# Cross-attention with a feed-forward block: k and the values projected in three f32r products, and the steps of a feed-forward row in another order

## The chip, the cores and the metric

The kernel runs on one core of a Trainium2 chip. The metric is the device time of one execution in microseconds (us), read as the median of several runs of the same program; lower is better.

## The reference

Eight sequences (b) of 512 rows of x and 512 rows of ctx, 256 features each. First a cross-attention with 16 heads of 16 features, then a feed-forward whose inputs and weights are rounded to a blockwise 4-bit grid:

```python
q = (layernorm(x) @ w_q.T + b_q)            # 8 x 512 x 256
k = ctx @ w_k.T + b_k
v = ctx @ w_v.T + b_v
scores = einsum('bthd,bshd->bhts', q * 0.25, k) + attn_bias   # 8 x 16 x 512 x 512
attn = softmax(where(mask, -big, scores))
x = x + (einsum('bhts,bshd->bthd', attn, v) @ w_out.T + b_out)
y = layernorm(x)
h = silu(fp4(y) @ fp4(w_gate).T) * (fp4(y) @ fp4(w_up).T)      # 704 wide
x = x + fp4(h) @ fp4(w_down).T
```

`fp4` divides every block of 16 values by its largest magnitude over 6, rounds to the grid 0, 0.5, 1, 1.5, 2, 3, 4, 6 and multiplies back. All inputs and outputs are float32.

## The kernel before, in words

Every engine has its instruction stream written out by hand; semaphores tie them together, and no scheduler reorders anything. The program has two stages.

**Attention.** An outer walk over the 8 batches, each in 32 steps `S_` (0 to 31; two halves of 16 steps, one for each group of 8 heads). In a step, TensorE makes two tiles of scores (`scores`, L1289: one f32r product of 128x512), transposes the two tiles that are four steps older (`transpose_tile`, through `transposes`, L1198: four 128x128 blocks each), and in every fourth step multiplies four older groups of probabilities by the values (`values`, L1335). Between these stand the small products of the batch. `heavy` (called after each pair of a score tile and a transposed tile) places one piece of a projection in most steps: the values in steps 0 to 7 (`make_v`, L1230), q of the next batch in steps 8 to 11 and 24 to 27 and k in steps 14, 15 and 28 to 31 (`make_qk`, L1220), the output projection of the batch before in steps 16 to 23 (L1253). A piece is one float32 product of 128x256, which the trace shows as two matmul records. `light`, at the end of a step, places the transposes of 4 blocks: of normalised x (`make_tx`), of ctx (`make_tc`, steps 9 and 13), of the attention output (`make_ot`, `make_oT`). They use PSUM banks M0 and M1 in turn, and each waits until the bank's last reader has it out.

VectorE takes the scores out of PSUM with the bias, mask and row maximum (L1060), ScalarE takes the transposed tiles out with the exponential (`exp_tile`, L767) and does a part of the subtractions (`less_max`, L774), GpSimd does the rest (L611). ScalarE also empties PSUM after the small products: `take_tc` (L713), `take_tx` (L708), `take_q` (L718), `take_k` (L723). In `step(b, S_)` these stand between the two exponentials of the step. A score tile waits until VectorE has taken the tile three before it; a transposed tile waits for the exponential of the tile two before it. `prob` is a ring of 14 tiles between L1060 and the transposes.

**Before the first score** k and q of the first heads are made in this order: transposes of ctx, weights and x on TensorE, copies out of them on ScalarE and VectorE (L780, L1043), projections, `high_k`/`high_q` on VectorE, the low parts on GpSimd, and then 24 small DMAs (`first_rows`, L393) from the queues of SyncE and ScalarE. ScalarE's copy of the value weights (L793) stands behind its 8 DMAs. VectorE then clears two slots of `stack` (L1046).

**Feed-forward.** 32 rows of 128 tokens, in `ffn_step(n)` on TensorE and ScalarE and `step(n)` on VectorE and GpSimd, as a pipeline over rows. TensorE in step n: transposes of the rounded h of row n-3 (L1198), gate and up of row n as 18 f32r products (L1529 to L1531: 12 of 128x512, 6 of 128x384), transposes of the rounded x of row n+1 (L1540), half of the down products of row n-3 (L1546, 6 records), one f32r product that makes the low part of x of row n+1 (L1556), the other half (6 records). ScalarE in step n: normalise row n+2 (`x_norm`, L862 and L866), copy of the transposed h (L890), `x_abs` of row n+2 (L882), silu of row n (L897), `x_parts` of row n+1 (L872 the high part, which L1556 waits for, and L875 the low part, which waits for L1556), absolute values of h of row n-1 (L904). VectorE's fourteen instructions of a step are L1128 to L1180, GpSimd has one (L692).

The middle rows run in a hardware loop of six steps a turn, four turns (`row_tiles`); the rest is written out.

## Time and profile before

| | before |
|---|---|
| median of 3 runs | 956.67 us (955.68 to 958.33) |
| profiled execution: its time / span from first to last instruction | 957.63 us / 955.8 us |
| mean granted TensorE clock | 0.991 |
| TensorE matmul busy | 900.2 us, 94% |
| TensorE weight loads busy | 707.5 us, 74% |
| VectorE busy | 715.0 us, 75% |
| ScalarE busy | 612.0 us, 64% |
| GpSimd busy | 534.8 us, 56% |

The times of all terms below are compared with the profiled execution: 957.63 us lie 0.96 us above the median. A matmul's busy time in the trace includes its way through the array, so that two neighbours overlap; how long TensorE is taken by an instruction is read from the distance of starts, not from its duration. Scores run from 25.9 us to about 661 us, the feed-forward rows from about 678 us to the end.

### The profile page before, as it was taken

To read this page: it belongs to the slowest core of one execution; us is meant where nothing else is said; L and a number is where in the kernel's file an instruction comes from. 1 tells how busy PE (TensorE), PEld (TensorE's weight loads), DVE (VectorE), ACT (ScalarE), POOL (GpSimd) and SP (SyncE) were. 2 spreads that over 40 slices of the span, in tenths; PEclk is the share of its full clock that TensorE was granted. 3 is DMA by queue.
4 is the path that set the end of the run, shared out by engine and by line. 5 is a ranking of instruction groups with operands and counts; after the bars stand their busy time and mean duration, and the time that the engine had idled before them with its cause. 6 is when DMAs were issued, how large, how long until landed. Compare 5 with 4: busy or idle time off the path is not lost.

```text
span 955.8 us, 20207 instructions
## 1 busy us (share of the span) xinstructions
PE 900.2 (94%) x6740; PEld 707.5 (74%) x6740; DVE 715.0 (75%) x1848; ACT 612.0 (64%) x1116; POOL 534.8 (56%) x500
## 2 busy tenths in 40 slices
PE   5799999999999999999999999898889999999997
PEld 4667778777777777777777777676667777777786
DVE  5867667677676766676766698996578888888884
ACT  3477767777777677776777778878445544444442
POOL 6777867867776686686777558854022222222222
PEclk9899999999999999999999999999989999999999
DMA  6586434334342443433435244300000000000000
GB/s 197 167 237 166 122 88 105 109 71 122 100 115 68 110 123 78 115 98 83 117 95 124 67 109 141 87 2 1 2 0 17 17 17 16 16 16 16 16 16 28
DMA packets 50792, 76.45 MB, mean 80 GB/s; under 512 B 5264, under 2 KB 22032, under 8 KB 50704
## 3 DMA queue, kind: packets, MB, share of 16 engines
q1 hardware_dynamic: 50448, 75.06, 29.5%
q8 instruction: 50, 0.82, 0.4%
q10 hardware_dynamic: 256, 0.26, 0.1%
q14 instruction: 38, 0.31, 0.1%
HBM read 45.16 MB, written 29.36 MB: 78 GB/s over the span
## 4 chain that ended last, share of the span: by engine, by line
PE 62%; issue 15%; ACT 10%; DVE 8%; POOL 1%; SPq 1%; DMA 1%; DVEq 0%; ACTq 0%; POOLq 0%
PE psum L1198 25%; PE psum L1335 12%; PE psum L1289 12%; PE psum L1220 5%; PE psum L1253 3%; PE psum L1230 2%; DVE att L1167 2%; ACT att L897 2%; ACT att L767 2%; ACT att L866 1%; ACT att L862 1%; DVE att L1138 1%; ACT att L774 1%; DVE att L1151 1%; PE psum L1556 1%
## 5 line engine op out<-in xcount | busy, mean ns | idle before, releaser
L1060 DVE CUSTOM_DVE_ANT_0 att<-psum,att 128x512 f32<-128x512 f32 x512 | 343.7, 687 | 167.4 <-PE psum L1289 166.3
L611 POOL TENSOR_TENSOR att<-att,neg_max 128x512 f32<-128x512 f32 x308 | 323.2, 1060 | 178.8 <-DVE neg_max L1060 176.2
L1198 PE MATMUL psum<-ident,att 128*128 128x128 f32 x2576 | 380.1, 275 | 24.9 <-ACT att L767 12.2
L1198 PEld LDWEIGHTS psum<-ident,att 128*128 128x128 f32 x2576 | 308.5, 141 | 95.6 <-ACT att L767 29.8
L767 ACT ACTIVATE att<-psum 128x512 f32<-128x512 f32 x512 | 299.3, 599 | 124.6 <-PE psum L1198 120.2
L1289 PE MATMUL psum<-stack 128*128 128x512 f32 x512 | 269.7, 528 | 8.5 <-DMA stack<-q_hl 6.0
L692 POOL TENSOR_TENSOR att<-att 128x704 f32<-128x704 f32 x32 | 61.6, 1927 | 182.9 <-DVE att L1176 182.9
L774 ACT ACTIVATE att<-att,neg_max 128x512 f32<-128x512 f32 x204 | 147.0, 721 | 10.3 <-DVE neg_max L1060 10.3
L1289 PEld LDWEIGHTS psum<-stack 128*128 128x128 f32 x512 | 97.7, 191 | 43.0 <-issue 31.1
L1335 PE MATMUL psum<-att 128*32 128x256 f32 x2048 | 123.8, 382 | 0.0
L1546 PE MATMUL psum<-att 128*128 128x256 f32 x384 | 92.9, 380 | 2.7 <-ACT att L890 2.7
L1335 PEld LDWEIGHTS psum<-att 128*32 128x32 f32 x2048 | 59.9, 109 | 44.6 <-issue 9.0
L882 ACT ACTIVATE att<-att 128x256 f32<-128x256 f32 x32 | 13.3, 417 | 102.6 <-DVE att L1172 102.6
L1546 PEld LDWEIGHTS psum<-att 128*128 128x128 f32 x384 | 68.5, 190 | 10.3 <-ACT att L890 3.4
L1529 PE MATMUL psum<-stack,q_hl 128*128 128x512 f32 (+1 forms) x192 | 75.6, 394 | 0.5 <-ACT q_hl L875 0.5
L1220 PE MATMUL psum<-att 128*128 128x256 f32 x256 | 74.9, 383 | 0.5
L1531 PE MATMUL psum<-stack,q_hl 128*128 128x512 f32 (+1 forms) x192 | 72.4, 377 | 0.0
L1530 PE MATMUL psum<-w_gu_low,q_hl 128*128 128x512 f32 (+1 forms) x192 | 72.3, 376 | 0.0
L1060 DVE DVE_READ_ACCUMULATOR2_ANT neg_max<- 128x1 f32 x512 | 42.2, 82 | 0.0
L1220 PEld LDWEIGHTS psum<-att 128*128 128x128 f32 x256 | 39.7, 191 | 2.9 <-ACT att L713 2.1
L730 ACT ACTIVATE att<-psum 128x512 f32<-128x512 f32 x32 | 19.1, 598 | 34.5 <-PE psum L1335 34.5
L595 POOL TENSOR_TENSOR att<-att 128x512 f32<-128x512 f32 x32 | 41.1, 1290 | 0.0
(98 smaller groups left out, 1023.0 us busy)
## 6 DMA issues: line engine op xcount, KB each, us to landing
stack<-qk_planes SPq DMA_DIRECT2D x124, 192.0 KB, 4.0
qk_planes<-k_hl SPq DMA_DIRECT2D x48, 256.0 KB
qk_planes<-q_hl SPq DMA_DIRECT2D x48, 256.0 KB
att<-in_fside_1xSxS_dram SPq DMA_DIRECT2D x32, 256.0 KB, 2.8
att<-in_ctx_dram SPq DMA_DIRECT2D x8, 512.0 KB, 6.6
out_dram<-att SPq DMA_DIRECT2D x32, 128.0 KB, 1.7
x<-in_x_dram SPq DMA_DIRECT2D x1, 2560.0 KB, 13.1
x<-in_x_dram SPq DMA_DIRECT2D x3, 512.0 KB, 7.7
```

Of the source, the lines that this page charges most:

```text
L611: pool.tensor_tensor(prob[:, slot, :], prob[:, slot, :], neg_max[:, slot:slot + 1].to_broadcast([P, S]), ALU.subtract).then_inc(less_pool, 1)
L767: act.activation(probT[:, u % 2, 2 * kk + r, :, (tt % 2) * P:(tt % 2 + 1) * P], src.rearrange("p (c t) -> p c t", c=SC), ACT.Exp, scale=1. ...
L774: act.activation(prob[:, slot, :], prob[:, slot, :], ACT.Identity, bias=neg_max[:, slot:slot + 1], scale=-1.0).then_inc(less_act, 1)
L1060: dve.tensor_tensor_reduce(out=prob[:, slot, :], in0=ps_score[:, SCORE_BANK[2 * S_ + r], :], in1=bias_m[:, tt, :], scale=-1.0, scalar=BIG, ...
L1198: return pe.transpose(out_, in_, ident[:, :])
L1220: last = pe.matmul(bank[:, cols], w_inT[:, c, which * E + o * P:which * E + (o + 1) * P], src[:, c, cols], start=c == 0, stop=c == EC - 1)
L1289: pe.matmul(ps_score[:, SCORE_BANK[j], :], stack[:, quad % SLOTS, kk, r, tt * P:(tt + 1) * P], stack[:, quad % SLOTS, kk, 2, :], start=Tru ...
L1335: last = pe.matmul(ps_O[32 * j:32 * j + 32, half * 2 * P:(half + 1) * 2 * P], vv[:, o, c, col:col + 2 * D], probT[:, u % 2, j, c, :], star ...
L1529: pe.matmul(ps_gu[:, c0:c1], f_xqT_high[:, par, c, :], w_gu_high[:, c, c0:c1], start=c == 0, stop=False)
L1530: pe.matmul(ps_gu[:, c0:c1], f_xqT_high[:, par, c, :], w_gu_low[:, c, c0:c1], start=False, stop=False)
L1531: last = pe.matmul(ps_gu[:, c0:c1], f_xqT_low[:, par, c, :], w_gu_high[:, c, c0:c1], start=False, stop=c == EC - 1)
L1546: last = pe.matmul(ps_y[:, 1 - par, :], f_hqT[:, 1 - par, c, :], w_dnT[:, c, :], start=c == 0, stop=c == IC - 1)
```

## The change

1. **k and the values.** ctx transposed and the weights of k and v are kept as a high part (rounded to f32r by ScalarE's copy) and a low part (what VectorE subtracts, `low_tc` and three subtractions at the start). A product of them is made as high x high + low x high + high x low, each an f32r product. k takes 6 products of 128x512 in the places of 4 float32 products of 128x256, a piece of `make_v` takes 3 f32r products of 128x256 in the place of one float32 product. q, the output projection and the down projection are unchanged.
2. **Places.** The second transposition of ctx moves from step 13 to step 11 and from bank M0 to M1; it waits for VectorE's low part of the first. `make_ot` moves from step 10 to step 12 and to bank M0, its `normalise` from step 11 to step 13 (in all batches but the last). `take_tc` of the second half moves from step 14 to step 12.
3. **Feed-forward.** ScalarE's step becomes: copy of the transposed h, `x_norm` of row n+3 (was n+2), silu, `x_abs` of row n+2, `x_high` of row n+1, absolute values of h, `x_low` of row n+1. VectorE's fourteen instructions stay the same and stand in another order. The loop makes three turns instead of four.
4. **Memory.** The ring of `prob` has 13 tiles instead of 14. `w_gu_low` shares the memory of the new high and low parts, `w_dnT` that of the q weights; GpSimd clears one block of it at the start.

```diff
-    RING = 14
+    RING = 13
...
-            return range(-2, 6), (6, ROWS - 2), range(ROWS - 2, ROWS + 4)
+            return range(-2, 6), (6, ROWS - 8), range(ROWS - 8, ROWS + 4)
...
             act.wait_ge(wT_ready, 2)
-            act.activation(w_inT[:, 1, 0:2 * E], psum[:, 1, :], ACT.Copy).then_inc(wT_taken, 1)
+            for c in range(EC):
+                act.activation(w_qT[:, c, :], psum[:, c, 0:E], ACT.Copy)
+                act.activation(w_kv_high[:, c, 0:E], psum[:, c, E:2 * E], ACT.Copy).then_inc(wk_high, 1)
...
-                    if S_ == 14 and not last:
-                        take_tc(b + 1, 1, M0)
+                    if S_ == 12 and not last:
+                        take_tc(b + 1, 1, M1)
...
             def ffn_step(n, par):
-                x_norm(n + 2, par)
...
-                if live(n + 2):
-                    x_abs(n + 2, par)
+                x_norm(n + 3, 1 - par)
...
+                if live(n + 2):
+                    x_abs(n + 2, par)
                 if live(n + 1):
-                    x_parts(n + 1, 1 - par)
+                    x_high(n + 1, 1 - par)
...
+                if live(n + 1):
+                    x_low(n + 1, 1 - par)
...
+            def low_tc(bp, i, bank):
+
+                dve.wait_ge(tc_taken, 2 * bp + i + 1)
+                dve.tensor_tensor(ctxT_low[:, i, :], bank, ctxT_high[:, i, :].bitcast(F32), ALU.subtract).then_inc(tc_low, 1)
...
             layernorm_stats(0, (0, 1, 2, 3))
+            for i in range(2):
+                low_tc(0, i, psum[:, 4 + i, :])
             layernorm_apply(0, (0, 1, 2, 3))
...
+            dve.wait_ge(wv_high, 1)
+            dve.tensor_tensor(w_kv_low[:, :, E:2 * E], psum[:, 1, :].rearrange("p (c e) -> p c e", c=EC), w_kv_high[:, :, E:2 * E].bitcast(F32),
+                              ALU.subtract).then_inc(wv_low, 1)
             dve.memset(stack[:, 1:SLOTS, :, :, :].bitcast(F32), 0.0).then_inc(stack_zero2, 1)
...
+                    if S_ in (10, 12) and not last:
+                        low_tc(b + 1, S_ // 12, M1)
...
+                    for j in ((0, 1), (2,), (3, 4), (5,))[piece]:
+                        c = j // 3
+                        w, y = ((w_kv_high, ctxT_high), (w_kv_high, ctxT_low), (w_kv_low, ctxT_high))[j % 3]
+                        last = pe.matmul(bank, w[:, c, o * P:(o + 1) * P], y[:, c, :], start=j == 0, stop=j == 5)
...
-                last = pe.matmul(bank[:, x * E:(x + 1) * E], ctxT[:, c, s * P:(s + 1) * P], w_inT[:, c, 2 * E:3 * E],
-                                 start=c == 0, stop=c == EC - 1)
+                for j in range(3):
+                    y, w = ((ctxT_high, w_kv_high), (ctxT_high, w_kv_low), (ctxT_low, w_kv_high))[j]
+                    last = pe.matmul(bank[:, x * E:(x + 1) * E], y[:, c, s * P:(s + 1) * P], w[:, c, E:2 * E],
+                                     start=c == 0 and j == 0, stop=c == EC - 1 and j == 2)
...
-                if S_ == 10 and not first:
+                if S_ == 11 and not last:
+                    pe.wait_ge(tc_low, 2 * b + 3)
+                    make_tc(b + 1, 1, M1)
+                if S_ == (10 if last else 12) and not first:
                     if last:
                         pe.wait_ge(v_taken, 2 * b + 2)
                     else:
-                        pe.wait_ge(tc_taken, 2 * b + 3)
-                    make_ot(4 * b - 1, M1)
-                if S_ == 13 and not last:
-                    pe.wait_ge(q_taken, 2 * b + 3)
-                    make_tc(b + 1, 1, M0)
+                        pe.wait_ge(q_taken, 2 * b + 3)
+                    make_ot(4 * b - 1, M1 if last else M0)
...
-            pe.wait_ge(wT_taken, 2)
-            pe.wait_ge(tc_taken, 2)
+
+            pe.wait_ge(wk_low, 2)
+            pe.wait_ge(tc_low, 2)
```

**VectorE, one step in the middle of the feed-forward,** before and then with the change (of 14 instructions, 12 rows with those of the registers). L1134, L1141, L1131, L1138 and L1145 of the first list are L1163, L1167, L1171, L1183 and L1190 of the second: maximum of normalised x, maximum of h, and the three roundings of x of row n+1.

```order
L1128 TENSOR_TENSOR att<-att,psum 128x704
L1131 SCALAR_TENSOR_TENSOR att<-att 128x256
L1133 REGISTER_ALU
L1134 TENSOR_REDUCE psum<-att 128x16
L1138 SCALAR_TENSOR_TENSOR att<-att 128x256
L1141 TENSOR_REDUCE psum<-att 128x44
L1145 TENSOR_TENSOR att<-att 128x256
L1151 ISA
L1151 TENSOR_TENSOR att<-psum,x 128x256
L1160 TENSOR_SCALAR att<-psum 128x60
L1161 TENSOR_SCALAR att<-psum 128x60
L1163 RECIPROCAL att<-att 128x60
```

```order
L1160 TENSOR_TENSOR att<-att,psum 128x704
L1163 TENSOR_REDUCE psum<-att 128x16
L1167 TENSOR_REDUCE psum<-att 128x44
L1171 SCALAR_TENSOR_TENSOR att<-att 128x256
L1179 TENSOR_SCALAR att<-psum 128x60
L1180 TENSOR_SCALAR att<-psum 128x60
L1183 SCALAR_TENSOR_TENSOR att<-att 128x256
L1186 RECIPROCAL att<-att 128x60
L1190 TENSOR_TENSOR att<-att 128x256
L1197 TENSOR_TENSOR att<-psum,x 128x256
L1202 SCALAR_TENSOR_TENSOR att<-att 128x704
L1207 TENSOR_TENSOR att<-att 128x256
```

The rounding of x (L1131, now L1171) moves behind both maxima, the scales and the reciprocal move ahead, and the residual sum (L1151, now L1197) moves behind the scaling of x.

**ScalarE, one step in the written-out end of the feed-forward,** before and with the change. L862/L866 (now L874/L878) are `x_norm`, L890 (L903) the copy of h, L882 (L896) `x_abs`, L897 (L909) silu, L872 (L884) and L875 (L889) the high and low part of x, L904 (L918) the absolute values of h.

```order
L866 ACTIVATE att<-att,rstd 128x256
L890 ACTIVATE att<-psum 128x768
L882 ACTIVATE att<-att 128x256
L897 ACTIVATE att<-psum 128x704
L872 ACTIVATE q_hl<-psum 128x256
L875 ACTIVATE q_hl<-psum 128x256
L904 ACTIVATE att<-att 128x704
```

```order
L903 ACTIVATE att<-psum 128x768
L874 ACTIVATE att<-x,neg_mean 128x256
L878 ACTIVATE att<-att,rstd 128x256
L909 ACTIVATE att<-psum 128x704
L896 ACTIVATE att<-att 128x256
L884 ACTIVATE q_hl<-psum 128x256
L918 ACTIVATE att<-att 128x704
L889 ACTIVATE q_hl<-psum 128x256
```

Normalising moves behind the copy of h and one row ahead, `x_abs` moves behind the silu, and the low part of x moves to the end of the step.

**ScalarE, steps 12 and 13 of a middle batch,** before and with the change. L767 (now L776) is an exponential, L774 (L783) a subtraction, L718 (L727) `take_q`, L713 (L722) `take_tc`.

```order
L718 ACTIVATE att<-psum,b_q 128x512
L774 ACTIVATE att<-att,neg_max 128x512
L767 ACTIVATE att<-psum 128x4x128 x4
L713 ACTIVATE att<-psum 128x512
L774 ACTIVATE att<-att,neg_max 128x512
```

```order
L727 ACTIVATE att<-psum,b_q 128x512
L722 ACTIVATE kv_hl<-psum 128x512
L783 ACTIVATE att<-att,neg_max 128x512
L776 ACTIVATE att<-psum 128x4x128 x4
L783 ACTIVATE att<-att,neg_max 128x512
```

The copy of ctx, which stood in step 14, now stands directly behind `take_q` and ahead of the second exponential of step 12.

## Rows read from the trace of the kernel before

**Rows 1.** Busy time by stretch: length, PE, PEld, DVE, ACT, POOL, clock, DMA.
```profile
260.00:360.00 100.00, 98.92 (x854) 76.98 (x850) 68.80 (x205) 72.18 (x130) 73.68 (x70) 1.00 0.40 104
760.00:860.00 100.00, 95.04 (x482) 77.92 (x481) 87.87 (x172) 50.88 (x102) 25.32 (x13) 1.00 0.05 16
```

**Rows 2.** Timeline (start, duration, engine), VectorE, first instruction of rows 5 and 29.
```profile
729.13 0.89 DVE L1128 TENSOR_TENSOR att<-att,psum 128x704 f32<-128x704 f32 x1
923.29 0.89 DVE L1128 TENSOR_TENSOR att<-att,psum 128x704 f32<-128x704 f32 x1
```

**Rows 3.** Timeline, one feed-forward row, all engines; in brackets idle time and releaser.
```profile
762.80 0.84 PE L1198 MATMUL psum<-ident,att 128*128 128x128 f32 x6
763.39 0.47 PE L1529 MATMUL psum<-stack,q_hl 128*128 128x512 f32 x1
763.83 0.43 DVE L1134 TENSOR_REDUCE psum<-att 128x16 f32<-128x256 f32 x1 [0.84 <-ACT att L866]
767.30 0.38 PE L1540 MATMUL psum<-ident,att 128*128 128x128 f32 x2
767.52 1.46 PE L1546 MATMUL psum<-att 128*128 128x256 f32 x6
767.97 0.42 ACT L882 ACTIVATE att<-att 128x256 f32<-128x256 f32 x1 [3.47 <-DVE att L1172]
768.29 0.74 ACT L897 ACTIVATE att<-psum 128x704 f32<-128x704 f32 x1
769.35 0.39 PE L1556 MATMUL psum<-q_hl,neg_ident 128*128 128x256 f32 x1 [0.37 <-ACT q_hl L872]
769.46 1.17 PEld L1546 LDWEIGHTS psum<-att 128*128 128x128 f32 x6
769.58 1.46 PE L1546 MATMUL psum<-att 128*128 128x256 f32 x6
770.87 0.29 PE L1198 MATMUL psum<-ident,att 128*128 128x128 f32 x1
```

**Rows 4.** Groups by line and shape: count, busy us, mean ns, idle before.
```profile
L1220 PE MATMUL psum<-att 128*128 128x256 f32 x256 | 74.9, 383 | 0.5
L1531 PEld LDWEIGHTS psum<-stack,q_hl 128*128 128x128 f32 x192 | 36.4, 190 | 5.7
```

**Rows 5.** Timeline, TensorE, first scores of batches 3 and 4.
```profile
261.44 0.50 PE L1289 MATMUL psum<-stack 128*128 128x512 f32 x1
341.54 0.50 PE L1289 MATMUL psum<-stack 128*128 128x512 f32 x1
```

**Rows 6.** Timeline, batch 3, from step 10's last transposes to step 15.
```profile
287.62 0.42 PEld L1198 LDWEIGHTS psum<-ident,att 128*128 128x128 f32 x4 [0.31 <-ACT att L713]
291.85 0.50 PE L1289 MATMUL psum<-stack 128*128 128x512 f32 x1
...
294.50 1.08 ACT L767 ACTIVATE att<-psum 128x512 f32<-128x512 f32 x2
295.15 1.09 PE L1198 MATMUL psum<-ident,att 128*128 128x128 f32 x8 [0.79 <-ACT att L767]
295.99 0.48 PE L1289 MATMUL psum<-stack 128*128 128x512 f32 x1
298.98 0.48 PE L1289 MATMUL psum<-stack 128*128 128x512 f32 x1
```

**Rows 7.** Timeline before the first scores; ACTq is ScalarE's DMA queue.
```profile
7.99 2.14 DVE L941 TENSOR_SCALAR att<-x,mean_var,rstd 128x256 f32<-128x256 f32 x4 [1.43 <-POOL rstd L566]
8.48 0.60 ACT L713 ACTIVATE att<-psum 128x512 f32<-128x512 f32 x1 [0.26 <-PE psum L1198]
17.14 5.18 DVE L1046 MEMSET stack<- 128x6144 f32 x1 [1.23 <-issue]
20.98 0.60 ACT L793 ACTIVATE att<-psum 128x512 f32<-128x512 f32 x1 [5.53 <-issue]
26.79 0.69 DVE L1060 CUSTOM_DVE_ANT_0 att<-psum,att 128x512 f32<-128x512 f32 x1 [4.47 <-PE psum L1289]
```

More of the change, by code:

```diff
@@ L1076, in body @@
                         take_v(b, S_ // 4 - 1, (M0, M1)[S_ // 4 - 1])
-                    if S_ == 11 and not first:
-                        normalise(2 * b - 1, 1, 1, M1)
+                    if S_ == (11 if last else 13) and not first:
+                        normalise(2 * b - 1, 1, 1, M1 if last else M0)
                     if S_ == 13 and not last:
@@ L1351, in heavy @@
                     if piece == 0:
[L1352 to L1357 removed]
+                        pe.wait_ge(tc_low, 2 * b + 4)
                     make_qk(1, 0, piece, M1, k_ready)
```

102 lines of the change are left out of this document (53 added, 49 removed).

## The prediction

> **What bounds the kernel now.** First the busy time by stretch [rows 1]. From 260 to 360 us TensorE is busy 98.9 of 100 us, VectorE 68.8 and ScalarE 72.2: the attention stage is TensorE's. From 760 to 860 us, in the feed-forward, TensorE shows 95.0 and VectorE 87.9: which of them bounds a row must be read from one row. So the timeline second. A row lasts 770.87 - 762.80 = 8.07 us [rows 3], and the 24 periods between the first VectorE instruction of row 5 and that of row 29 take 923.29 - 729.13 = 194.16 us, 8.09 each [rows 2]. In the same row TensorE's own work, from start to start, is 0.59 (transposes of h) + 3.91 (gate and up) + 0.22 (transposes of x) + 1.29 (six down records) + 0.23 (L1556) + 1.29 (six more) = 7.53 us. The missing 0.54 us is one wait: the first six down records start at 767.52 and are through at 768.81, and L1556 starts at 769.35, released by ScalarE's L872. VectorE's share is 87.87 / (100 / 8.07) = 7.09 us a row, with one idle piece of 0.84 us, in which it waits for ScalarE's L866. Read together these are a ring: ScalarE's L904, then `x_norm`, then VectorE from L1134 to L1172, then ScalarE's L882, which has waited 3.47 us, then silu, L872, L1556, L875 and L904 again. Neither engine is the bound there; the order is.
>
> Third, a batch of attention: 341.54 - 261.44 = 80.10 us [rows 5], the same in all middle batches. Its waits are small and local; the largest stand in steps 10 to 14 [rows 6].
>
> **Feed-forward.** The new order cuts the ring in three places. Normalised x of the next step is made a row ahead, so VectorE's 0.84 us goes. `x_abs` stands behind silu and L872's copy no longer stands behind a late VectorE result: VectorE's step can begin when gate and up of row n-1 end, and its scaling of x (L1172, now L1207) is done when all but the last two of its fourteen instructions are, about 7.09 - 1.7 = 5.4 us later; the products of row n end 7.53 us after those of row n-1. So silu, `x_abs` and the high part follow each other at once: silu is released by the gate half, which ends six products of 384 columns (about 1.1 us) before the rest, takes 0.74 us [rows 3], `x_abs` then 0.42, and the high part is out about 0.8 us after the transposes of x start, while 0.22 + 1.29 us of TensorE work cover it. The low part moves to the end of ScalarE's step, some 2.3 us after the products end; it is needed 3.6 us after them. GpSimd's multiplication ends about 8.5 us after its VectorE step began and is needed at 10.6. A row becomes 7.53 us. Next in line is VectorE with 7.09 us: a margin of 0.44. **Gain 0.54 x 26 rows = 14.0 us** (24 measured periods and two at the ends; the first rows, among the last products of attention, and the drain of three rows I leave as they are). Bounds: 0.3 a row (8 us) if a new wait takes half of it, 0.6 x 29 (17 us) if the first rows gain too. Three loop turns instead of four cost nothing visible: the written-out rows run at the same pace.
>
> **k.** A float32 product of 128x256 is two records of 0.215 us (256 records on L1220 for 128 products [rows 4]; six records in 1.29 us [rows 3]), 0.43 in all; four of them 1.72 us. An f32r product is read from gate and up: 12 x 512 + 6 x 384 = 8448 columns in 3.91 us, 0.463 ns a column, so 0.237 us for 512. Six take 1.42: 0.30 less for each k. Of the two in a batch, the one in steps 14 and 15 gives it; the one in steps 28 to 31 stands over ScalarE, whose chain of two exponentials, `take_q` or `take_oT` and a subtraction already makes TensorE wait there a little, so I count nothing. **0.30 x 7 = 2.1 us.**
>
> **The values.** 8 pieces a batch, each 3 f32r products of 256 columns instead of 0.43 us. The trace has one such product, L1556, whose successor starts 0.23 us later, but it comes after a wait, so its weights are loaded in the open: the successor's load starts 0.11 us after it (769.46) and its matmul 0.12 after that [rows 3]. A load of 128 columns thus takes 0.11 to 0.12, as long as 256 columns at 0.463 ns (0.12). Behind one another, with loads under matmuls, I take 0.125: a piece 0.375, 0.055 less, eight pieces 0.44, of which a third falls on steps that end on a wait for ScalarE. **0.3 x 8 = 2.4 us.** Bounds: 0.11, the pace of the 128-column transposes (two in 0.22, each with its load under the other [rows 3]), gives 0.8 a batch, 6 us; 0.23, L1556 as it stands, gives 24 x 0.23 = 5.52 against 3.44, a loss of 2.1 a batch, 17 us. I take the value near the low end since a stream of products is like gate and up, not like a lone one.
>
> Gate and up load 18 stationary tiles, each a record of 190 ns [rows 4], in 3.91 us: there is no room in it for an open load of 0.11 at every product. The skill, page TensorE: Matmul & The Clock Gate, in its part on row and column tiling, says that weight loads overlap matmuls in flight only when they go to another row group. By that rule the products of k and v, all on the full 128 rows, would each pay their load, and the sum would be the third rival's, 964 us; the trace of before disagrees with it at gate and up.
>
> **Moved steps.** In a middle batch: step 10 loses `make_ot` (0.44, four transposes at 0.11) and the 0.31 us wait for `take_tc` (287.62). Step 11 gains `make_tc`, 0.44; VectorE's low part, due at the end of step 10 plus 0.6 + 0.7 us, is there before it. Steps 12 and 13 now take 295.99 - 291.85 = 4.14 us; the second transposed tile of step 13 waits for the exponential that ScalarE starts at 294.50 after `take_q`. `take_tc` now stands before it and takes 0.5 more (two exponentials, also 128x512 out of PSUM, take 1.08 together); `make_ot` has moved into the wait for q in step 12, `make_tc` has gone from step 13. So that tile starts at 295.65, and with its 0.44 the pair takes 4.24: 0.10 more. Step 14 (295.99 to 298.98, 2.99) has 2 x 0.237 + 8 x 0.11 + 2 x 0.43 + 0.44 = 2.65 of work; its rest, a wait on `take_tc`, goes. Sum -0.75 + 0.44 + 0.10 - 0.34 = -0.55. **0.55 x 6 = 3.3 us** in batches 1 to 6; batch 0 has no `make_ot` and loses 0.15. VectorE's two `low_tc` are 1.4 us a batch of an engine that is 69% busy; the three score banks hide them. Ring of 13: a tile waits for the transposes of the tile 13 before; TensorE has issued those of the tile 9 before when it makes the score. Nothing.
>
> **Before the first score.** VectorE now makes both low parts of ctx ahead of the normalisation: the second copy of ScalarE ends at 8.48 + 0.60, the subtraction takes 0.69 as every 128x512 out of PSUM, so L941 starts at 9.8 instead of 7.99. TensorE has the transposes of x ahead of k, k itself is 0.3 shorter: k, the 16 DMAs of SyncE behind it and the first score come 1.5 us later. ScalarE's copy of the value weights (20.98) stands behind its DMAs, which wait on k and q: 22.5. VectorE's subtraction now waits for it ahead of the 5.18 us memset: 22.5 + 0.6 + 0.7 + 5.2 = 29.0, up to 30.2 with the 1.23 us issue gap, where L1060 began at 26.79 [rows 7]. The first steps run at VectorE's pace, so this stays. **Cost 2.5 us**, between 1.5 and 3.4.
>
> **Sum.** -14.0 - 2.1 - 2.4 - 3.3 + 0.15 + 2.5 = -19.2. 957.63 - 19.2 = 938.4 for a profiled execution, 0.96 less for the median: 937.5, rounded 938.
>
> **Rivals.**
> 1. *VectorE takes over the feed-forward.* A row's 8.07 us hold 7.09 of VectorE work and 0.98 of gaps; if the new order only moves those gaps (an instruction that now stands ahead of its operand waits instead of L1134), a row stays at 8.0 and the stage gains 2 us, not 14: 950. For it: a margin of only 0.44. Against: in the new order another instruction stands between every two that depend on each other, and by the times above each operand from another engine is early. 12%.
> 2. *Loads in the open in the values only.* 0.23 a product: +2.1 instead of -0.3 a batch, 19 us back: 957, no change. For it the one row of this form; against it gate and up. 7%.
> 3. *Loads in the open in k too (slower).* Each product pays 0.11: k takes 6 x 0.347 = 2.08 against 1.72, +0.36 x 15 + 2.1 = 7.5 more: 964. It decides from 0.066 us above the hidden pace: 19 us over 36 products x 8. 6%.
> 4. *The first feed-forward rows speed up as well and the low bound of the values holds*: 930. 5%.
>
> **Chances.** My forecast has 70%, its own range 931 to 946. The range 930 to 951 takes in rivals 1 and 4 and leaves out 2 and 3. A measurement of this kernel tells apart about 0.3%, 2.9 us: faster (below 953.8) is the forecast, rivals 1 and 4, 87%; within it rival 2, 7%; slower rival 3, 6%.
>
> **What would show it.** Right: feed-forward rows 7.5 to 7.6 us apart, no idle time before the product after the first six down records; k's products 0.24 and v's 0.12 to 0.13 apart; a middle batch of about 79.0 us; first L1060 at 29 to 30. Wrong: VectorE without idle time in the feed-forward (rival 1), weight loads between v's matmuls with starts 0.23 apart (2, 3), or a wait of TensorE for the low part of ctx in step 11 or 14.

## The result: 930.87 us, and the profile after

| | before | after |
|---|---|---|
| median | 956.67 us (3 runs, 955.68 to 958.33) | 930.87 us (4 runs, 929.18 to 931.13) |
| ratio to before, 95% interval | | 0.9724 [0.9702, 0.9746] |
| profiled execution: time / span | 957.63 / 955.8 us | 930.9 / 928.9 us |
| TensorE matmul, share of the span | 94% | 95% |
| VectorE, ScalarE, GpSimd, share | 75%, 64%, 56% | 76%, 67%, 58% |

A fourth run of the kernel before took 1137.72 us and is left out of the median and of the ratio. Faster by 25.8 us, and 7 us under the 938 of the forecast: just inside the range of 930 to 951, and 0.1 us below the 931 at which the forecast's own range began. The two spans differ by 26.9 us. Cut at the first score of each batch (TensorE) and at the first VectorE instruction of a feed-forward row, in the traces of both kernels:

| stretch | before | after | difference | forecast |
|---|---|---|---|---|
| start to first score | 25.9 | 28.3 | +2.4 | +2.5 (with the first steps) |
| batch 0 | 75.4 | 77.1 | +1.8 | −0.45 |
| batches 1 to 5, each | 80.09 | 78.85 | −1.24 (5 x: −6.2) | −1.15 (5 x: −5.8) |
| batch 6 | 81.75 | 82.00 | +0.25 | −1.15 |
| batch 7 to its last score | 77.0 | 77.0 | 0 | −0.3 |
| last score to row 0 | 23.4 | 22.0 | −1.4 | 0 |
| rows 0 to 5 | 45.2 | 37.1 | −8.1 | 0 |
| rows 5 to 29 (24 periods) | 194.2 | 177.7 | −16.5 | −13 |
| rows 29 to 31 | 13.3 | 14.8 | +1.5 | −1 |
| row 31 to the end | 19.2 | 18.6 | −0.6 | 0 |

The feed-forward, with the approach to its first row, gave 25.1 us where 14.0 were forecast, attention with its start 1.8 where 5.2 were forecast.

**The feed-forward.** First the busy time of the kernel after in the two stretches of [rows 1]; the columns are the same.

```profile
260.00:360.00 100.00, 98.83 (x877) 77.17 (x879) 71.11 (x211) 73.70 (x133) 75.25 (x72) 1.00 0.41 107
760.00:860.00 100.00, 100.00 (x528) 87.84 (x527) 90.28 (x187) 57.30 (x109) 27.28 (x14) 1.00 0.05 18
```

In the attention stretch nothing visible changes: TensorE was full and is full. In the feed-forward the 5 us of gaps are gone; TensorE is now the bound there too, with VectorE at 90. Then one row of the kernel after, from the timeline (start, duration, engine, line; in brackets idle time and what ended it), to be laid beside [rows 3]:

```profile
770.69 0.19 PEld L1594 LDWEIGHTS psum<-q_hl,neg_ident 128*128 128x128 f32 x1
770.71 0.47 PE L1594 MATMUL psum<-q_hl,neg_ident 128*128 128x256 f32 x1
770.90 1.17 PEld L1584 LDWEIGHTS psum<-att 128*128 128x128 f32 x6
771.02 1.46 PE L1584 MATMUL psum<-att 128*128 128x256 f32 x6
772.31 0.82 PE L1233 MATMUL psum<-ident,att 128*128 128x128 f32 x6
772.88 0.47 PE L1567 MATMUL psum<-stack,q_hl 128*128 128x512 f32 x1
775.93 0.76 ACT L909 ACTIVATE att<-psum 128x704 f32<-128x704 f32 x1 [0.84 <-PE psum L1569]
776.79 0.38 PE L1578 MATMUL psum<-ident,att 128*128 128x128 f32 x2
776.99 0.89 DVE L1160 TENSOR_TENSOR att<-att,psum 128x704 f32<-128x704 f32 x1 [0.70 <-PE psum L1569]
777.01 1.46 PE L1584 MATMUL psum<-att 128*128 128x256 f32 x6
777.21 0.38 ACT L884 ACTIVATE q_hl<-psum 128x256 fp32r<-128x256 f32 x1 [0.22 <-PE psum L1578]
778.12 0.47 PE L1594 MATMUL psum<-q_hl,neg_ident 128*128 128x256 f32 x1
778.42 1.46 PE L1584 MATMUL psum<-att 128*128 128x256 f32 x6
```

L1594 (L1556 before) to L1594 is 778.12 − 770.71 = 7.41 us. The wait before it is gone: the high part L884 is out at 777.59, half a microsecond early. The idle time of VectorE and of ScalarE now ends on TensorE, on gate and up (L1569); before it ended on ScalarE and on VectorE. The weights of L1594 are loaded at 770.69, while the down products ahead of it still run, and those of its successor at 770.90, ahead of that matmul at 771.02. Its own start is not a good mark, since its record begins before the sixth down record has run its 0.215 us. What it adds is read from the two groups of down products around it: the second starts 778.42 − 777.01 = 1.41 us after the first, six records take 1.29 of it, and the product has the other 0.12, where it stood 0.23 before its successor in [rows 3].

The first instruction of VectorE in rows 0, 5, 29 and 31 of the kernel after (rows 5 and 29 of before are [rows 2]; rows 0 and 31 of before start at 683.9 and 936.6):

```profile
680.73 0.89 DVE L1160 TENSOR_TENSOR att<-att,psum 128x704 f32<-128x704 f32 x1 [1.15 <-PE psum L1569]
...
717.84 0.89 DVE L1160 TENSOR_TENSOR att<-att,psum 128x704 f32<-128x704 f32 x1 [0.78 <-PE psum L1569]
...
895.50 0.89 DVE L1160 TENSOR_TENSOR att<-att,psum 128x704 f32<-128x704 f32 x1 [0.69 <-PE psum L1569]
...
910.31 0.89 DVE L1160 TENSOR_TENSOR att<-att,psum 128x704 f32<-128x704 f32 x1 [1.53 <-PE psum L1569]
```

Rows 0 to 5 took 10.99, 8.62, 8.19, 9.51 and 7.94 us before and take 9.74, 6.52, 6.51, 6.85 and 7.49: 45.2 against 37.1. TensorE's granted clock differs here too. The columns are again those of [rows 1]; the first line is the third of these rows before, the second the same row after, the third the same row in old_vector_order, a run below:

```profile
703.49:711.68 8.19, 7.20 (x27) 6.00 (x27) 6.73 (x14) 3.95 (x7) 2.32 (x2) 0.63 0.00 0
696.99:703.50 6.51, 5.50 (x30) 4.76 (x31) 6.38 (x13) 4.10 (x9) 1.96 (x2) 1.00 0.00 0
694.80:702.36 7.56, 6.42 (x27) 5.47 (x27) 6.65 (x14) 3.73 (x7) 2.72 (x2) 0.77 0.00 0
```

Before, TensorE stood idle for 2.50 us (700.67 to 703.17, a wait for ScalarE's L872), the granted clock was 0.5 from 702.71 to 709.54, and the gate and up products of 512 columns started 0.43 us apart in it and 0.23 behind it. Another such stretch is 685.64 to 689.06. The kernel after has none in its feed-forward.

**Attention.** First scores of batches 3, 4, 6 and 7 after ([rows 5] are those of batches 3 and 4 before), then those of batches 6 and 7 before:

```profile
263.16 0.50 PE L1331 MATMUL psum<-stack 128*128 128x512 f32 x1
...
342.00 0.50 PE L1331 MATMUL psum<-stack 128*128 128x512 f32 x1
...
499.70 0.50 PE L1331 MATMUL psum<-stack 128*128 128x512 f32 x1
...
581.70 0.50 PE L1331 MATMUL psum<-stack 128*128 128x512 f32 x1
```

```profile
501.73 0.50 PE L1289 MATMUL psum<-stack 128*128 128x512 f32 x1
...
583.48 0.50 PE L1289 MATMUL psum<-stack 128*128 128x512 f32 x1
```

A middle batch takes 78.84, near the forecast (79.0). Steps 12 to 15 of batch 3 after, beside [rows 6]:

```profile
294.97 0.60 ACT L722 ACTIVATE kv_hl<-psum 128x512 fp32r<-128x512 f32 x1
296.06 1.09 ACT L776 ACTIVATE att<-psum 128x512 f32<-128x512 f32 x2
296.72 0.66 PE L1233 MATMUL psum<-ident,att 128*128 128x128 f32 x4
297.13 0.48 PE L1331 MATMUL psum<-stack 128*128 128x512 f32 x1
299.62 0.48 PE L1331 MATMUL psum<-stack 128*128 128x512 f32 x1
```

The second transposed tile of step 13 (296.72) comes behind the exponential that follows the copy of ctx (L722), as the forecast had it; step 14 takes 299.62 − 297.13 = 2.49 against 2.99. Steps 10 to 15 together take 16.83 against 17.69: step 10 takes 0.73 less, step 11 0.49 more, steps 12 and 13 0.05 more, steps 14 and 15 0.67 less.

**The start.** Timeline of the kernel after, beside [rows 7]:

```profile
23.42 0.60 ACT L804 ACTIVATE kv_hl<-psum 128x512 fp32r<-128x512 f32 x1 [5.52 <-issue]
25.97 5.18 DVE L1075 MEMSET stack<- 128x6144 f32 x1 [1.23 <-issue]
28.33 0.77 PE L1331 MATMUL psum<-stack 128*128 128x512 f32 x1 [7.17 <-DMA stack<-q_hl]
31.07 0.63 DVE L1089 CUSTOM_DVE_ANT_0 att<-psum,att 128x512 f32<-128x512 f32 x1
```

VectorE's first maximum (L1060 before, L1089 now) starts at 31.07, 4.3 us later than before and 1 to 2 later than forecast; it is the memset that it stands behind.

### The profile page after: what moved, and what is told of

Same layout as the page of the kernel before. It is cut to its first block, busy times and chain, and to the rows that moved or that the text cites. A ratio compares the mean times of both kernels' runs of the same rounds, so it can differ in the third digit from the quotient of the medians.

```text
span 928.9 us, 20211 instructions
## 1 busy us (share of the span) xinstructions
PE 883.6 (95%) x6772; PEld 706.7 (76%) x6772; DVE 710.6 (76%) x1866; ACT 617.8 (67%) x1119; POOL 534.8 (58%) x501
## 4 chain that ended last, share of the span: by engine, by line
PE 79%; ACT 6%; issue 6%; DVE 4%; POOL 2%; DMA 2%; SPq 1%; ACTq 0%; DVEq 0%
PE psum L1233 26%; PE psum L1377 11%; PE psum L1331 11%; PE psum L1584 9%; PE psum L1569 4%; PE psum L1568 4%; PE psum L1567 4%; PE psum L1295 3%; PE psum L1255 2%; ACT att L776 2%; DVE att L1089 2%; PE psum L1261 2%; ACT att L783 1%; PE psum L1272 1%; ACT att L727 1%
## 5 line engine op out<-in xcount | busy, mean ns | idle before, releaser
L1089 DVE CUSTOM_DVE_ANT_0 att<-psum,att 128x512 f32<-128x512 f32 x512 | 341.7, 686 | 143.3 <-PE psum L1331 141.4
L776 ACT ACTIVATE att<-psum 128x512 f32<-128x512 f32 x512 | 298.3, 599 | 117.7 <-PE psum L1233 113.4
L1331 PE MATMUL psum<-stack 128*128 128x512 f32 x512 | 251.2, 492 | 10.5 <-DMA stack<-q_hl 7.2
L783 ACT ACTIVATE att<-att,neg_max 128x512 f32<-128x512 f32 x204 | 147.2, 722 | 13.4 <-DVE neg_max L1089 13.4
L1584 PE MATMUL psum<-att 128*128 128x256 f32 x384 | 91.7, 380 | 2.7 <-ACT att L903 2.7
L1584 PEld LDWEIGHTS psum<-att 128*128 128x128 f32 x384 | 68.4, 190 | 10.9 <-ACT att L903 3.4
L1569 PE MATMUL psum<-stack,q_hl 128*128 128x512 f32 (+1 forms) x192 | 72.1, 376 | 0.0
L1568 PE MATMUL psum<-kv_hl,q_hl 128*128 128x512 f32 (+1 forms) x192 | 71.9, 375 | 0.0
L903 ACT ACTIVATE att<-psum 128x768 f32<-128x768 f32 x32 | 26.0, 814 | 53.4 <-PE psum L1233 53.4
L909 ACT ACTIVATE att<-psum 128x704 f32<-128x704 f32 x32 | 24.3, 760 | 38.1 <-PE psum L1569 38.1
L1160 DVE TENSOR_TENSOR att<-att,psum 128x704 f32<-128x704 f32 x32 | 28.4, 888 | 23.2 <-PE psum L1569 22.8
L1089 DVE DVE_READ_ACCUMULATOR2_ANT neg_max<- 128x1 f32 x512 | 42.1, 82 | 0.0
L1567 PEld LDWEIGHTS psum<-stack,q_hl 128*128 128x128 f32 x192 | 36.1, 188 | 6.3 <-ACT q_hl L889 0.8
```

The source lines that it names most:

```text
L776: act.activation(probT[:, u % 2, 2 * kk + r, :, (tt % 2) * P:(tt % 2 + 1) * P], src.rearrange("p (c t) -> p c t", c=SC), ACT.Exp, scale=1. ...
L783: act.activation(prob[:, slot, :], prob[:, slot, :], ACT.Identity, bias=neg_max[:, slot:slot + 1], scale=-1.0).then_inc(less_act, 1)
L1089: dve.tensor_tensor_reduce(out=prob[:, slot, :], in0=ps_score[:, SCORE_BANK[2 * S_ + r], :], in1=bias_m[:, tt, :], scale=-1.0, scalar=BIG, ...
L1331: pe.matmul(ps_score[:, SCORE_BANK[j], :], stack[:, quad % SLOTS, kk, r, tt * P:(tt + 1) * P], stack[:, quad % SLOTS, kk, 2, :], start=Tru ...
L1567: pe.matmul(ps_gu[:, c0:c1], f_xqT_high[:, par, c, :], w_gu_high[:, c, c0:c1], start=c == 0, stop=False)
L1568: pe.matmul(ps_gu[:, c0:c1], f_xqT_high[:, par, c, :], w_gu_low[:, c, c0:c1], start=False, stop=False)
```

## The experiments

"Ratio" is to the kernel before, timed beside it, with its 95% interval. All edits are to the kernel after, unless another is named.

**The two halves of the change apart.** The kernel before with the new order of ScalarE's and VectorE's feed-forward step alone (as item 3 of the change):

> The kernel before with the new feed-forward order alone (ScalarE's and VectorE's steps and the loop bounds); k and the values stay float32. Theory A: the gain of the change is the feed-forward's, and it does not need the rest: rows 7.41 us apart as in the changed kernel, first rows 6.5 to 6.9 apart, the attention stage as before (batches 80.1 us). The two traces give the feed-forward 25 us of the 27, so 932.5 us (931 to 934). Rival B: the fast first rows come from the other part (banks, memory, an earlier end of attention): rows 7.41 apart but the first ones at 8 to 9 as before, 940 us.

933.44 us (932.59 to 933.72, 4 runs), ratio 0.9762 [0.9747, 0.9777]. Rows 7.41 us apart, first rows 9.74, 6.51, 6.51, 6.84, batches 80.08. So 23.3 us of 25.8 are the order, and the row's 7.41 has nothing to do with k and the values.

The counterpart: the kernel after with the old order of both engines in the feed-forward.

> The changed kernel with the feed-forward order of before: k and the values in f32r, moved steps, ring of 13. Theory A: middle batches 78.85 us, but 4.2 us are lost before the first maximum and in batch 0, and batch 6 gains nothing; sum -1.8 us: 955.5 (954 to 957). Rival B (the sum of the prediction for this stage, -5): 952. Feed-forward rows at 8.07 us in both.

954.45 us (11 runs, 950.09 to 956.28), ratio 0.9969 [0.9952, 0.9985]. Batches 78.83, batch 0 77.14, batch 6 81.95, rows 8.07. The products, the moved steps and the dearer start give 2.3 us; 23.3 + 2.3 is the whole within the spread of the runs, so no action of the halves on each other is to be seen.

**Which engine's order.** VectorE's step back to the old order, ScalarE's new:

> The changed kernel with VectorE's feed-forward step in the order of before; ScalarE keeps the new order. Theory A: the ring is cut on ScalarE alone (normalised x a row ahead, x_abs behind silu), and VectorE's order only saves waits between dependent neighbours: rows 7.4 to 7.5 us, 931 to 935 us. Rival B: both orders are needed, rows stay near 8.0: 945 to 950 us.

931.13 us (930.71 to 933.34, 4 runs), ratio 0.9744 [0.9728, 0.976]; rows 7.41. In the middle rows VectorE's new order gives nothing. It gives something in the first: rows 1 to 5 take 6.64, 7.56, 7.38 and 7.51 us where the new order has 6.52, 6.51, 6.85 and 7.49, so 38.8 us from row 0 to 5 instead of 37.1. In the third of these rows, 7.56 us long, the granted clock was 0.77 (third line of the group above): 0.23 x 7.56 = 1.7 us of full clock are missing, as much as the whole difference, so all of it may go by way of the clock. From row 31 to the end the old order takes 19.2 us and the new one 18.6; up to row 0 the old one is 0.5 shorter. The time does not show the sum of 1.9 us, since the first score of this profile stood at 26.52 and not at 28.33 (see the last section). The other way round, ScalarE's step back:

> The changed kernel with ScalarE's feed-forward step in the order of before; VectorE keeps the new order. Theory A: the ring is whole again and longer, since in the new order more VectorE work stands between the maximum of x and its scaling (about 4.5 us where it was 4.1): rows 8.4 to 8.6 us, first rows slow too, 955 to 965 us. Rival B: VectorE's new order does a part of the work by itself: rows 7.6 to 8.0, 938 to 948 us.

959.4 us (955.46 to 960.79, 10 runs), ratio 1.0024 [1.0006, 1.0041]; rows 8.28 us apart, longer than before though short of the 8.4 to 8.6 expected: the ring is closed, and the new order of VectorE makes it longer. Its timeline, VectorE's maximum of x in two rows, `x_abs` (L893) and the product of the low part between them:

```profile
800.99 0.43 DVE L1156 TENSOR_REDUCE psum<-att 128x16 f32<-128x256 f32 x1 [1.34 <-ACT att L877]
...
805.34 0.42 ACT L893 ACTIVATE att<-att 128x256 f32<-128x256 f32 x1 [3.67 <-DVE att L1200]
...
806.73 0.39 PE L1587 MATMUL psum<-q_hl,neg_ident 128*128 128x256 f32 x1 [0.60 <-ACT q_hl L883]
...
809.27 0.43 DVE L1156 TENSOR_REDUCE psum<-att 128x16 f32<-128x256 f32 x1 [1.34 <-ACT att L877]
```

These are the waits of [rows 3], each longer: 1.34 for 0.84, 3.67 for 3.47, 0.60 for 0.37.

**Which link.** Three kernels, each with one of the three moves in ScalarE's step, VectorE's order new, the others old. They are read against old_scalar_order, 8.28 a row. Normalised x a row ahead alone:

```diff
                 x_norm(n + 3, 1 - par)
+                if live(n + 2):
+                    x_abs(n + 2, par)
...
-                if live(n + 2):
-                    x_abs(n + 2, par)
                 if live(n + 1):
-                    x_high(n + 1, 1 - par)
+                    x_parts(n + 1, 1 - par)
...
-                if live(n + 1):
-                    x_low(n + 1, 1 - par)
```

> The kernel of old_scalar_order (changed kernel, ScalarE's feed-forward step as before, rows 8.28 us) with one of the three moves: normalising a row ahead, behind the copy of h. Theory A: there is one ring and each move takes a link out of it; this one opens the ring altogether, so rows fall to TensorE's 7.41 us, 931 to 934 us. Rival B: the moves must come together, since each leaves a ring through the other two: rows above 7.8, over 943 us.

932.78 us (930.04 to 935.52, 2 runs), ratio 0.9753 [0.9716, 0.9791]; rows 7.41. This one move opens the ring whole in the middle; the first five periods take 40.0 us, 2.9 more than with all three moves. Two of them hold stretches at the lower clock (granted 0.85 over 11.02 us and 0.77 over 7.56), which is 3.4 us of full clock.

`x_abs` behind the silu alone:

```diff
             def ffn_step(n, par):
+                x_norm(n + 2, par)
...
-                x_norm(n + 3, 1 - par)
...
-                    x_high(n + 1, 1 - par)
+                    x_parts(n + 1, 1 - par)
...
-                if live(n + 1):
-                    x_low(n + 1, 1 - par)
```

> The kernel of old_scalar_order (rows 8.28 us) with x_abs behind silu alone. Theory A: the ring stays but loses its silu, 0.63 us from start to start: rows 7.6 to 7.7 us, 937 to 941 us. Rival B: rows above 7.9, since the wait only moves.

945.91 us (2 runs), ratio 0.9891 [0.987, 0.9911]; rows 7.85, not the 7.6 to 7.7 expected. Two rows of its timeline, ScalarE's low part and VectorE's maximum of x:

```profile
801.19 0.38 ACT L886 ACTIVATE q_hl<-psum 128x256 fp32r<-128x256 f32 x1 [0.69 <-PE psum L1587]
...
803.31 0.43 DVE L1156 TENSOR_REDUCE psum<-att 128x16 f32<-128x256 f32 x1 [0.91 <-ACT att L877]
```

The row is 0.43 shorter, but the low part still stands ahead of the absolute values and of the next `x_norm`, and waits 0.69 for its product; VectorE then waits 0.91 for the normalisation.

The low part last alone:

```diff
             def ffn_step(n, par):
+                x_norm(n + 2, par)
...
-                x_norm(n + 3, 1 - par)
+                if live(n + 2):
+                    x_abs(n + 2, par)
...
-                if live(n + 2):
-                    x_abs(n + 2, par)
```

> The kernel of old_scalar_order (rows 8.28 us) with the low part of x at the end of ScalarE's step alone. Theory A: the ring loses L1556's product and the low part, 0.8 us: rows 7.45 to 7.55 us, 932 to 937 us. Rival B: rows above 7.8.

952.67 us (3 runs), ratio 0.9953 [0.9935, 0.9971]; rows 8.07, where 7.45 to 7.55 were expected: a miss. Its timeline:

```profile
806.33 0.79 ACT L917 ACTIVATE att<-att 128x704 f32<-128x704 f32 x1 [0.27 <-DVE att L1213]
807.03 0.37 ACT L888 ACTIVATE q_hl<-psum 128x256 fp32r<-128x256 f32 x1
807.29 0.50 ACT L873 ACTIVATE att<-x,neg_mean 128x256 f32 x1
808.45 0.43 DVE L1161 TENSOR_REDUCE psum<-att 128x16 f32<-128x256 f32 x1 [1.13 <-ACT att L877]
```

The absolute values of h (L917) now come up before VectorE has them ready and wait 0.27; the low part (L888) still runs between them and the next `x_norm` (L873). The move shortens the ring by 0.21 and leaves it closed. What this run's theory overlooked is ScalarE's own order: an instruction moved to the end of a step still stands ahead of the first of the next.

**The products.** The values back to one float32 product each, ctx and weights taken unsplit in their high part (the low parts are made but left out of the values):

```diff
-                for j in range(3):
-                    y, w = ((ctxT_high, w_kv_high), (ctxT_high, w_kv_low), (ctxT_low, w_kv_high))[j]
-                    last = pe.matmul(..., y[:, c, s * P:(s + 1) * P], w[:, c, E:2 * E], ...)
+                last = pe.matmul(..., ctxT_high[:, c, s * P:(s + 1) * P].bitcast(F32), w_kv_high[:, c, E:2 * E].bitcast(F32), ...)
```

> The changed kernel with each piece of the values as one float32 product of the high parts (low parts of ctx and of the value weights left out of the values). Theory A: three f32r products of 256 columns take 0.36 us, one float32 product 0.43: steps 0, 2, 3, 4, 5 and 7 get 0.07 to 0.09 us longer, and steps that end on a wait for ScalarE do not: middle batches 79.2 to 79.4, time 934. Rival B (weights loaded in the open in f32r): the batch gets shorter with float32: below 78.5, 927.

931.29 us (930.13 to 932.08), ratio 0.973 [0.9711, 0.9749]. A middle batch takes 79.23: the values are worth 0.38 us a batch (forecast 0.3). The time does not show it, since this execution's first score came 1.6 us earlier than that of the kernel after (see the last section), against 2.8 us more in batches 0 to 6.

k back to four float32 products in the same way:

> The changed kernel with k as four float32 products of the high parts (low parts of ctx and of the k weights left out of k). Theory A: k in steps 14 and 15 costs 0.3 us more, k in steps 28 to 31 next to nothing, since those steps end on a wait for ScalarE: middle batches 79.1 to 79.2, time 932.5 to 933.5. Rival B: both cost 0.3 us: batches 79.45, 935.5.

932.05 us (931.72 to 933.4), ratio 0.9741 [0.9723, 0.9759]. A middle batch takes 79.17, 0.32 more (forecast 0.30), all of it in steps 14 and 15; steps 28 to 31 take 9.79 with either kind of product, as forecast. What is left of the 1.24 us of a middle batch, 1.24 − 0.38 − 0.32 = 0.54, falls to the moved steps (forecast 0.55). No run has them alone, but the traces agree by step: −0.73 in step 10, +0.49 in 11, +0.05 in 12 and 13, and −0.35 in 14 and 15 once k's 0.32 is taken off, where the forecast had −0.75, +0.44, +0.10 and −0.34.

A piece of the values in the kernel after, between four transposed blocks and the next score:

```profile
263.50 0.60 PE L1233 MATMUL psum<-ident,att 128*128 128x128 f32 x4
263.85 0.61 PE L1272 MATMUL psum<-kv_hl 128*128 128x256 f32 x3
264.30 0.39 PE L1331 MATMUL psum<-stack 128*128 128x512 f32 x1
```

From the first block to the score 0.80 us pass. The four blocks take 4 x 0.109 = 0.44 of it, by the distance of their starts; the three products have the other 0.36, 0.12 each, without idle time. (The starts inside a piece are uneven, 0.20 and 0.12 apart, since the record of its first product begins 0.03 after that of the last block.)

**Batch 6 and the start.** In batch 6 VectorE waits for the first piece of w_down. Its timeline there, and the DMA that brings it:

```profile
536.87 3.15 SPq L439 DMA_DIRECT2D att<-in_L_ffn_w_down_dram  x3
...
544.02 0.69 DVE L1039 TENSOR_REDUCE w_am<-att 128x32 f32<-128x512 f32 x1 [1.47 <-DMA att<-in_L_ffn_w_down_dram]
```

Before, the DMA was issued at 538.54, and the same instruction started at 545.76 with no such wait. Step 16 began at 543.50 before and at 540.21 after: it came 3.3 us earlier, the DMA only 1.7. The work on the weights begun one step later:

```diff
-        WEIGHT_BEGIN = [(B - 2, 16), (B - 2, 20), ...
+        WEIGHT_BEGIN = [(B - 2, 17), (B - 2, 20), ...
```

> The changed kernel with VectorE's first look at the feed-forward weights one step later (batch 6, step 17 instead of 16). Theory A: batch 6 takes 82.0 us where the others take 78.85, and gained nothing from the change, because the attention steps became shorter than the DMA of the first weights, which VectorE now waits 1.5 us for: batch 6 takes 80.3 to 80.8, the time is 929.5 us or so. Rival B: VectorE has too much work there whatever comes first: batch 6 stays at 81.7 to 82.2, time 931.

927.43 us (927.2 to 927.57), ratio 0.9697 [0.968, 0.9713]: 3.4 us under the kernel after; batch 6 takes 80.15 for 82.0. That is 1.85 of it, by the mechanism of its theory and a little more than its 80.3 to 80.8; 1.5 more is the earlier start, the first score of its profile at 26.84 and not at 28.33.

VectorE's low part of the value weights behind its memset, and with it the ring of `prob` cut from 13 to 11 tiles:

```diff
-    RING = 13
+    RING = 11
...
+            dve.memset(stack[:, 1:SLOTS, :, :, :].bitcast(F32), 0.0).then_inc(stack_zero2, 1)
             dve.wait_ge(wv_high, 1)
             dve.tensor_tensor(w_kv_low[:, :, E:2 * E], ..., ALU.subtract).then_inc(wv_low, 1)
-            dve.memset(stack[:, 1:SLOTS, :, :, :].bitcast(F32), 0.0).then_inc(stack_zero2, 1)
```

> The changed kernel with VectorE's subtraction for the value weights behind the memset instead of ahead of it, and a ring of 11 tiles instead of 13. Theory A: the subtraction waits for ScalarE's copy behind eight DMAs, and the memset of 5.2 us behind it: VectorE starts on the scores 1.5 to 2.5 us sooner, batch 0 is VectorE's at first, so 929 us; and the ring never binds, middle batches stay at 78.85 us. Rival B: the first scores wait for their DMAs anyway: under 0.5 us gained. Rival C: the ring binds: middle batches longer, VectorE waiting on transposes.

927.67 us (926.6 to 928.18), ratio 0.9693 [0.9674, 0.9711]. Its timeline at the start:

```profile
18.00 5.18 DVE L1072 MEMSET stack<- 128x6144 f32 x1 [1.23 <-issue]
...
27.64 0.69 DVE L1089 CUSTOM_DVE_ANT_0 att<-psum,att 128x512 f32<-128x512 f32 x1 [3.92 <-issue]
```

The first maximum starts at 27.64 for 31.07, and batch 0 takes 74.77 for 77.14: 2.4 us, which is what the wait ahead of the memset cost. Middle batches stay at 78.85 with a ring of 11: there the ring does not bind at 13, or at 11. Batch 7 took 78.26 for 77.00 in this profile: VectorE waits 3.55 us in it for the DMA of w_gate, which landed 9.2 us after its issue and 7.1 to 7.3 us in the kernels before, after, weights_step_17 and start_and_weights. Why it landed late, no run shows.

**Both together,** and the normalisation ahead of the low parts of ctx (RING stays 13):

```diff
             layernorm_stats(0, (0, 1, 2, 3))
+            layernorm_apply(0, (0, 1, 2, 3))
             for i in range(2):
                 low_tc(0, i, psum[:, 4 + i, :])
-            layernorm_apply(0, (0, 1, 2, 3))
```

> The changed kernel with three edits that the runs point to: the memset ahead of the subtraction for the value weights, the normalisation of x ahead of the low parts of ctx before the first score, and VectorE's first look at the feed-forward weights in step 17 of batch 6. Theory A: 3.5 us from the third as measured, 1.5 to 2.5 from the first, about 0.7 from the second: 925 us (923.5 to 926.5). Rival B: the first two give nothing because the first scores wait for DMAs: 927.4.

925.37 us (924.98 to 926.55, 5 runs), ratio 0.9677 [0.9661, 0.9693]; batch 0 74.76, batch 6 80.16. It is the fastest of all, 0.6% under the kernel after. Its first score starts at 27.12, later than in memset_first_ring11 (26.73) and weights_step_17 (26.84): no gain from the normalisation is to be seen.

## Why the prediction was right, and where it was short

**The ring, right.** The one wait of 0.54 us in a row was read as a ring, not as an engine at its limit. norm_ahead_only and old_scalar_order show it: the same instructions on every engine, 7.41 or 8.28 us a row by ScalarE's order alone. "The new order cuts the ring in three places" credits too much: one place, normalising a row ahead, is enough, each of the other two alone leaves it closed (7.85 and 8.07), and VectorE's order does nothing for a middle row (old_vector_order, 7.41).

**The size of a row, 0.12 too long.** The term that was mis-sized is "0.23 (L1556)" in the sum of 7.53. I took it over from the row with the wait, though the prediction itself says two paragraphs on that this row pays its load in the open because it follows a wait. Without the wait the load goes under the sixth down record, and the product costs 0.12. That makes 7.53 − 0.11 = 7.42, measured 7.41, and the rows 5 to 29 give 16.5 us instead of 24 x 0.54 = 13.0: 2.9 from the 0.12, the rest from the period of 8.09 that stood beside the row of 8.07.

**The first rows, left out: 8.1 us.** "the first rows, among the last products of attention, and the drain of three rows I leave as they are" is the term that was mis-sized most. The down products of row n − 3 are missing in the first steps, so TensorE has less to do there; before, the second to fourth of these rows took 8.2 to 9.5 us all the same, and with the new order 6.5 to 6.9. ffn_order_only shows it with the batches untouched. In the rows of 6.5 VectorE's instructions follow one another without a wait in the trace (busy 6.38 us, TensorE 5.50 in the row shown above), so its work sets them. Two things held these rows before, and no run takes them apart: the waits of the ring, and the lower clock behind TensorE's longer waits. The stretches at 0.5 last 3.4 and 6.8 us, so at most half of 10.2, 5.1 us by this estimate, goes with the clock. In all seven profiles with both engines' new order the granted clock stays 1.00 from row 0 to row 5; in the other seven it falls there. norm_ahead_only (40.0) and old_vector_order (38.8) are among those seven, and they lose in the first rows and not in the middle. The bound named for this, 0.6 x 29 = 17 us, fell short of the 25.1 measured, since it gave a first row the gain of a middle one.

**The two ends of the feed-forward.** The 1.4 us between the last score and row 0 come with `x_abs` behind the silu: 22.0 us in abs_behind_silu_only as in the kernel after, 23.5 in norm_ahead_only, low_last_only and old_scalar_order. At the other end rows 29 to 31 cost 1.5 us more than before, and row 31 to the end 0.6 less, so the two end periods that were counted in the 26 give nothing. The 0.6 is VectorE's order: 18.6 us in every run that has it, 19.2 in old_vector_order, kv_only and the kernel before. Why the periods from 29 to 31 were 6.6 and 6.7 us before and are 7.41 after no run here took apart.

**k, the values, the moved steps: right in a middle batch, over-counted beyond.** 0.32, 0.38 and 0.54 against 0.30, 0.3 and 0.55. But "0.30 x 7", "0.3 x 8" and "0.55 x 6" took every batch for a middle one. Batch 6 gained nothing: its step 16 came 3.3 us earlier, the DMA of the weights 1.7, and VectorE stood 1.47 us before it with the maxima of the scores behind it (weights_step_17: 1.85 us). Batch 7, without q and k of a next batch, gained nothing either: 77.0 both times; VectorE's wait there for the DMA of w_gate is 1.72 us for 0.87 before, which fits, but no run moved it. These are 1.4 + 0.3 = 1.7 us that did not come; the batches 1 to 5 gave 0.4 more than forecast.

**The start, right in kind, 2.15 short.** The forecast had the wait of the memset and the price of 2.5 with 3.4 at the high end; first score and batch 0 cost 2.4 + 1.8 = 4.2, and the 0.45 that batch 0 was to gain did not come either. ScalarE's copy (L804) was 0.9 later than the forecast's 22.5. In this profile the transposes of x and k's products ran at half pace (last section), 0.8 and 1.2 us longer than in old_vector_order. With them at full pace, as in weights_step_17, the first score stands at 26.84 and the first maximum at 29.56, where the forecast had 29 to 30: 1.5 of the 2.15 are this slow start. Batch 0 is 77.1 us long either way, with 7.0 us of it at the lower granted clock (kv_only) or with 11.1 (weights_step_17), so the clock does not price it; the memset does.

**Together,** against the forecast: rows 5 to 29 3.5 more, the first rows 8.1, the approach to row 0 1.4, the end 2.0 less (+0.9 where −1.1 stood), which makes 11.1 more from the feed-forward; start and batch 0 2.15 less, batches 6 and 7 1.7 less, batches 1 to 5 0.4 more, which makes 3.4 less from attention. That is 7.7 us of span; 0.2 us more than before lie outside the span, and 7.5 us are left between 938.4 and 930.9. The two errors have opposite signs, and that the time fell inside the stated range is in part luck: with attention as forecast it would have been 3.4 us lower, 927.5, and below the range.

**Rivals.** VectorE as the bound (950): refuted, its idle time ends on gate and up, 0.70 us a row. Open loads in the values (957) and in k too (964): refuted by products that take 0.12 us in the values and 0.23 in k (at full pace, last section), and by v_float32 and k_float32, which are slower by batch. The rule of the Trainium skill that stood beside the third rival (page TensorE: Matmul & The Clock Gate, on row and column tiling) is that loads overlap matmuls in flight only for another row group. As that sentence stands the trace disagrees: these products use all 128 rows, the records of their loads last 190 to 200 ns each, and a product still takes 0.12 us. A sentence above it in the same part of the page also lets a load be pulled ahead when it goes to the background weight buffer; that fits the trace. The fourth rival (930) came out in its number and half in its mechanism: the first rows speed up, by more than twice the 3 us it allowed, but the values gain 0.38 us a batch and not the 0.8 of their low bound.

## What to carry to other kernels

Where no engine is full and a row still does not get shorter, follow the waits around until they close: this ring was opened by moving one instruction a turn ahead, and a move that only shortens a wait inside it gave a quarter or a half of it here. Count the fill rows for themselves: they waited too, with less work in them than in the middle, and TensorE's granted clock fell behind the waits. After a gain in each turn look for what keeps its own time, here a DMA begun at a fixed step and a copy ahead of a long memset: two such edits gave 1.85 and 2.4 us in their batches.

## What the runs showed of the hardware that was not expected

A matmul's load costs by what stands ahead of it. The f32r product of 128x256 that makes the low part of x costs 0.23 us behind a wait (L1556) and 0.12 in a full stream (L1594, the same product); those of the values (L1272) cost 0.12 as well.

k's six products before the first score ran at two paces in profiles of nearly the same code. The kernel after, then old_vector_order:

```profile
11.03 1.97 PE L1233 MATMUL psum<-ident,att 128*128 128x128 f32 x8 [1.00 <-DVE att L959]
12.65 2.79 PE L1261 MATMUL psum<-kv_hl 128*128 128x512 f32 x6
```

```profile
11.15 1.09 PE L1229 MATMUL psum<-ident,att 128*128 128x128 f32 x8 [1.00 <-DVE att L959]
12.00 1.64 PE L1257 MATMUL psum<-kv_hl 128*128 128x512 f32 x6
```

From the second of the six on, 512 columns take 0.427 us in the first and 0.22 to 0.24 in the second. TensorE had idled 1.00 us for VectorE's normalisation just before in both. The first pace is that of a stretch with a granted clock of 0.5 (1.2 GHz), where gate and up of the kernel before also start 0.427 apart (706.9 to 709.1 us); the second is that of 2.4 GHz.

